# A graph attention layer with a mixer and a routed feed-forward block: the weighted sums over edges take pairs of neighbouring tiles, one accumulator, and one-hots that read their columns from PSUM

## The reference

```python
scores = einsum('ehd,ehd->eh', Q[dst], K[src] + 0.2 * rel[:, None, :]) / D ** 0.5
ex = exp(scores - segment_max(scores, dst)[dst])
denom = segment_sum(ex, dst)
agg = segment_sum(ex / denom[dst] * V[src], dst)      # 4 heads of 64
msgs = where(deg > 0, agg, V)
x = x + layernorm(msgs @ Wo + bo + xn) * gamma + beta + mixer(xn)
```

## Time and profile before

| | us |
|---|---|
| three runs: median | 2975.46 |
| lowest, highest | 2974.98, 2976.96 |
| the profiled execution: its time | 2994.86 |
| its span, first to last instruction | 2993.0 |
| first and last matmul of the weighted sums (start) | 1772.6, 2233.8 |
| mean granted TensorE clock, of full speed | 0.840 |

### The profile page before, as it was taken

How to read it: one execution, slowest core, us unless ns; L and a number is a source line. 1 busy time by engine, 2 the same in 40 slices (tenths; PEclk the granted TensorE clock), 3 DMA queues, 4 the chain that set the end, 5 groups by cost and what they waited for, 6 DMA issues and landing times. The chain is left out here.

```text
span 2993.0 us, 48887 instructions
## 1 busy us (share of the span) xinstructions
PE 2231.8 (75%) x11266; PEld 1389.1 (46%) x11267; DVE 1922.4 (64%) x3248; ACT 868.0 (29%) x2658; POOL 1478.5 (49%) x1460
## 2 busy tenths in 40 slices
PE   6863667666766766766676748999985999967997
PEld 3431333333333333333333436666654666546886
DVE  5653666666666666666666879999995666541111
ACT  2430011011101101100100177777761555531221
POOL 3555555555555555555555226666644434214442
PEclk9995777777777777777777779999997999978999
DMA  4545878787888788878778837777744444354541
GB/s 151 183 156 172 275 257 266 256 270 247 261 270 265 246 264 265 257 249 272 249 253 265 191 129 233 236 235 237 239 150 149 159 146 169 113 192 182 174 169 55
DMA packets 347414, 636.52 MB, mean 213 GB/s; under 512 B 36018, under 2 KB 224950, under 8 KB 347227
## 3 DMA queue, kind: packets, MB, share of 16 engines
q1 hardware_dynamic: 269259, 373.23, 37.9%
q0 software_dynamic: 77824, 262.55, 27.8%
q10 hardware_dynamic: 272, 0.00, 0.0%
HBM read 461.16 MB, written 175.42 MB: 213 GB/s over the span
## 5 line engine op out<-in xcount | busy, mean ns | idle before, releaser
L698 POOL DMA_INDIRECT s_kv<-kv_d,s_index x832 | 795.0, 956 | 657.6 <-issue 325.0
L829 PE MATMUL s_q_ps<-q,s_is_dst 128*128 x2496 | 511.7, 321 | 399.7 <-DVE s_key L752 272.5
L829 PEld LDWEIGHTS s_q_ps<-q,s_is_dst 128*128 128x128 bf16 x2496 | 210.6, 105 | 572.3 <-issue 506.5
L1190 PE MATMUL a_sum_ps<-a_w,a_is_dst 128*128 128x260 f32 x1664 | 421.8, 397 | 48.4 <-DVE odd_sums L1157 31.5
L748 DVE TENSOR_TENSOR s_key<-s_kv,s_rel_ps 128x1024 f32<-128x1024 f32 x208 | 252.4, 1214 | 230.1 <-remote 222.8
L1125 POOL TENSOR_TENSOR a_w<-a_v,a_w 128x512 f32<-128x512 f32 x208 | 284.7, 1369 | 225.2 <-ACT a_w L1095 173.0
L1190 PEld LDWEIGHTS a_sum_ps<-a_w,a_is_dst 128*128 128x128 f32 x1664 | 300.8, 190 | 169.3 <-DVE odd_sums L1157 123.2
L1103 ACT ACTIVATE a_w<-a_v,a_w 128x64 f32<-128x64 f32 x1248 | 319.9, 334 | 3.9 <-DMA a_v<-v_d 3.8
L834 PE MATMUL s_rel_ps<-rel,s_is_kind 64*128 64x64 bf16 x2496 | 244.7, 207 | 52.5 <-issue 51.9
L647 ACT COPY scores<-s_part 128x32 f32 (+1 forms) x104 | 22.6, 218 | 835.9 <-issue 708.6
L757 DVE TENSOR_REDUCE s_part<-s_key 128x16 f32<-128x1024 f32 x208 | 253.7, 1220 | 10.7
(11 more groups left out here) (295 smaller groups left out, 3030.4 us busy)
## 6 DMA issues: line engine op xcount, KB each, us to landing
v_d<-s_kv SPq DMA_DIRECT2D x208, 512.0 KB
a_v<-v_d SPq DMA_DIRECT2D x208, 512.0 KB, 5.3
s_local<-local_d SPq DMA_DIRECT2D x106, 256.0 KB
xh_d<-h_hid SPq DMA_DIRECT2D x24, 1024.0 KB, 6.9
s_kind<-type_d SPq DMA_DIRECT2D x212, 64.0 KB
s_kv<-kv_d,s_index POOLq DMA_INDIRECT x832
kv_d<-pkv SPq DMA_DIRECT2D x50, 256.0 KB, 2.0
wd<-in_L_ffn_Wd SPq DMA_DIRECT2D x8, 1024.0 KB, 12.2
```

The lines of the kernel that those rows point to most:

```text
L698: nc.gpsimd.indirect_dma_start(out=kv[:, g * GROUP + b, :], out_offset=None, in_=R["kv"], in_offset=bass.IndirectOffsetOnAxis(ap=index[:, ...
L829: nc.tensor.matmul(q_ps[b][:, u, :], is_dst[:, h, e], M["q3"][:, bass.ds(regs[g % GROUPS * GROUP + u], 1), j, :] .rearrange("p a c -> p (a ...
L1190: ins = nc.tensor.matmul(sum_ps[g % 2 * GROUP + u][:], is_dst[:, g % WRING, u, :], w[:, g % WRING, u, :], start=True, stop=True)
```

## The change

The unit of the weighted sums is now an *item*, two neighbouring tiles of one block; a block with an odd number of tiles gets an item whose second tile is the next block's. There is room for 440 items, so 220 groups of two items (880 tiles) where there were 208 of four tiles (832).

- Tile planning computes for each item its first tile and its block, by 15 small VectorE instructions that stand between the block table and the wait for the gathered edges, and stores both (`items`). TensorE turns the global node (`segment`) in place of `local`.
- `v_d` is laid out [partition, tile, 256] with room for 833 tiles, so that any two neighbouring tiles are 2 KB in a row of a partition. The scores stage writes the same 4 KB per partition and group, now 833 KB apart. The weighted sums load two tiles with each DMA, 256 KB, two DMAs per group, at an address from a register.
- The two matmuls of an item accumulate in one bank; there are four banks, and one add per item, always to `sums`. `odd`, its zeroing and the add at the end go.
- The one-hots are one instruction per tile, 128 x 128: column (from a copy in PSUM) minus global node, compared with minus the first node of the block. An edge of another block finds no column. Both scalars are addressed by registers.
- VectorE, ScalarE and SyncE load the item's tile numbers into registers in each group, two values at a time; VectorE has three such loads per group (blocks of group n, tiles and blocks of group n + 2), before it had one of four values.
- ScalarE multiplies two tiles in every fourth group and one in the others (before: in turn two and one), GpSimd the rest.
- The loops run over 27 times 8 groups, with 4 more behind.

```diff
--- before.py
+++ after.py
@@ -437,6 +451,9 @@
+            sp.wait_ge(S["items_set"], 2)
+            sp.dma_start(R["items"].rearrange("k (p c) -> p k c", p=IT_ROWS), item_i[:]).then_inc(S["table_in"], 16)
@@ -492,6 +511,26 @@
+            then(nc.vector.tensor_scalar(room_i[:], tiles[:], 1.0, None, ALU.add))
+            then(nc.vector.tensor_scalar(room_i[:], room_i[:], 1, None, ALU.arith_shift_right))
+            st.mark(nc.vector.memset(first_item[:, 0:1], 0.0))
+            then(nc.vector.tensor_copy(pairs[:], room_i[:]))
...
+            then(nc.vector.scalar_tensor_tensor(out=item_off[:], in0=first_item[:, 0:RBLK], scalar=-2.0,
...
+            then(nc.vector.scalar_tensor_tensor(out=item_tile[:], in0=item_no[:], scalar=2.0, in1=item_base[:],
+                                                op0=ALU.mult, op1=ALU.add))
+            nc.vector.tensor_scalar(item_i[:, 0, :], item_tile[:], float(T - 2), None, ALU.min).then_inc(S["items_set"], 1)
+            nc.vector.tensor_scalar(item_i[:, 1, :], item_blk[:], -1.0, None, ALU.add).then_inc(S["items_set"], 1)
@@ -525,7 +564,7 @@
-                x = src_f if b < 2 else local
+                x = src_f[:] if b < 2 else M["segment"][:].rearrange("p (t e) -> p t e", e=P)
@@ -610,8 +649,8 @@
-                        sp.dma_start(R["v"][bass.ds(i * (RING // 2) + h, 1)].rearrange("a p n -> (a p) n")
-                                     .rearrange("p (j c) -> p j c", c=C)[:, g % 2 * GROUP:(g % 2 + 1) * GROUP, :],
+                        sp.dma_start(R["v"][:, 0:T, :].rearrange("p (n u) c -> p n u c", u=GROUP)
+                                     [:, bass.ds(i * RING + g, 1)].rearrange("p a u c -> p (a u) c"),
@@ -948,14 +992,13 @@
-                zero(M["odd"], lo, hi)
+                zero(M["sums"], lo, hi)
...
-                zero(M["odd"], lo, hi)
-            zero(M["sums"], 0, RBLK)
+                zero(M["sums"], lo, hi)
@@ -1052,51 +1101,66 @@
...
-        TURNS = T // (VRING * GROUP)
+        PAIRS = GROUP // 2
+        BANKS = 4
+        NGROUP = ITEMS // PAIRS
+        TURNS, REST = NGROUP // VRING, NGROUP % VRING
...
-        sum_ps = [ctx.enter_context(nc.psum_tensor(f"a_sum_ps{b}", [P, AGG], F32)) for b in range(2 * GROUP)]
+        sum_ps = [ctx.enter_context(nc.psum_tensor(f"a_sum_ps{b}", [P, AGG], F32)) for b in range(BANKS)]
+        col_ps = ctx.enter_context(nc.psum_tensor("a_col_ps", [P, P], F32))
...
-        ACT_TILES = {g: range(0, 2 - g % 2) for g in range(VRING)}
-        POOL_TILES = {g: range(2 - g % 2, GROUP) for g in range(VRING)}
...
+        ACT_TILES = {g: range(0, 2 if g % 4 == 0 else 1) for g in range(VRING)}
+        POOL_TILES = {g: range(ACT_TILES[g].stop, GROUP) for g in range(VRING)}
...
+        tiles_of = lambda n: items[0:1, 0, bass.ds(n * PAIRS, PAIRS)]
+        blocks_of = lambda n: items[0:1, 1, bass.ds(n * PAIRS, PAIRS)]
...
+            at_tile = [sp.alloc_register(f"a_sp{k}") for k in range(PAIRS)]
+            def groups(i, count):
+                for g in range(count):
                     for name in ("pool_done", "act_done"):
                         sp.wait_ge(S[name], i * VRING + g + 1)
                     sp.nop(nofuse=True)
...
+                    regs = load_row(sp, at_tile, tiles_of(i * VRING + g), T - 2)
+                    for k in range(PAIRS):
+                        sp.dma_start(v[:, g, 2 * k:2 * k + 2, :], R["v"][:, bass.ds(regs[k], 2), :]).then_inc(v_in[g], 16)
...
+            def copy_scores(n, at):
+                regs = load_row(act, at_tile, tiles_of(n), T - 2)
+                for k in range(PAIRS):
+                    nc.scalar.copy(w[:, at, 2 * k:2 * k + 2, C:], scores[:, bass.ds(regs[k], 2), :]).then_inc(S["ex_ready"], 1)
...
+                        act.wait_ge(S["summed"], (n + 2) * PAIRS)
                         act.nop(nofuse=True)
...
+                        copy_scores(n + 1, (g + 1) % WRING)
+                    act.wait_ge(S["ex_ready"], (n + 1) * PAIRS)
+                    act.wait_ge(v_in[g], (i + 1) * (16 * PAIRS))
@@ -1105,100 +1169,104 @@
...
+            with pool.Fori(0, TURNS) as i:
+                groups(i, VRING)
+            groups(TURNS, REST)
...
+            nc.vector.tensor_copy(col_ps[:], M["col"][:]).then_inc(S["col_set"], 1)
...
-            dve.sem_inc(S["summed"], WRING)
...
+            dve.sem_inc(S["summed"], WRING * PAIRS)
...
-            def prepare(i, g):
...
-                dve.wait_ge(S["summed"], n + 1)
...
-                nc.vector.tensor_tensor(is_dst[:, g % WRING], M["col"][:, None, :].broadcast_to([P, GROUP, P]),
...
+            tile_at = [dve.alloc_register(f"a_tile{k}") for k in range(PAIRS)]
+            node_at = [dve.alloc_register(f"a_node{k}") for k in range(PAIRS)]
+            sums_at = [dve.alloc_register(f"a_sums{k}") for k in range(PAIRS)]
+            def ahead(n):
+                return (load_row(dve, tile_at, tiles_of(n), T - 2), load_row(dve, node_at, blocks_of(n), RBLK - 1))
+            def one_hot(at, k, tiles, blocks):
+                for u in range(2):
+                    ins = nc.vector.tensor_scalar(is_dst[:, at, 2 * k + u, :], col_ps[:],
+                                                  node_of[:, bass.ds(tiles[k] + u, 1)],
+                                                  M["first_node"][:, bass.ds(blocks[k], 1)], ALU.subtract, ALU.is_equal)
+                ins.then_inc(S["hot_done"], 1)
+            def groups(i, count, last):
+                for g in range(count):
                     n = i * VRING + g
-                    add(i, g, load_row(dve, at_block, M["blk"][0:1, bass.ds(n * GROUP, GROUP)], RBLK - 1))
+                    more = not (last and g + LEAD >= count)
+                    regs = load_row(dve, sums_at, blocks_of(n), RBLK - 1)
+                    if more:
+                        tiles, blocks = ahead(n + LEAD)
+                    for k in range(PAIRS):
+                        if more:
+                            dve.wait_ge(S["summed"], (n + LEAD + 1) * PAIRS)
+                            one_hot((g + LEAD) % WRING, k, tiles, blocks)
+                        j = n * PAIRS + k
+                        dve.wait_ge(S["summed"], j + 1 + WRING * PAIRS)
+                        dve.wait_ge(S["added"], j + BANKS)
+                        dve.nop(nofuse=True)
+                        at = sums[:, bass.ds(regs[k], 1), :].rearrange("p a c -> p (a c)")
+                        nc.vector.tensor_tensor(at, at, sum_ps[(g * PAIRS + k) % BANKS][:], ALU.add).then_inc(S["added"], 1)
...
-            dve.wait_ge(S["added"], T + 2 * GROUP)
-            nc.vector.tensor_tensor(sums[:], sums[:], odd[:], ALU.add).then_inc(S["whole"], 1)
...
+            with dve.Fori(0, TURNS) as i:
+                groups(i, VRING, False)
+            groups(TURNS, REST, True)
+            dve.wait_ge(S["added"], ITEMS + BANKS)
...
-                    pe.wait_ge(S["added"], n * GROUP + GROUP)
-                    for u in range(GROUP):
-                        ins = nc.tensor.matmul(sum_ps[g % 2 * GROUP + u][:], is_dst[:, g % WRING, u, :], w[:, g % WRING, u, :],
-                                               start=True, stop=True)
-                    ins.then_inc(S["summed"], 1)
+                    for k in range(PAIRS):
+                        pe.wait_ge(S["hot_done"], n * PAIRS + k + 1)
+                        pe.wait_ge(S["added"], n * PAIRS + k + 1)
+                        for u in range(2):
+                            ins = nc.tensor.matmul(sum_ps[(g * PAIRS + k) % BANKS][:], is_dst[:, g % WRING, 2 * k + u, :],
+                                                   w[:, g % WRING, 2 * k + u, :], start=(u == 0), stop=(u == 1))
+                        ins.then_inc(S["summed"], 1)
```

More of the change, by code:

```diff
@@ L37 @@
 T = TS_ROWS * TS_COLS
+ITEMS = 440
+IT_ROWS = 110
+IT_COLS = ITEMS // IT_ROWS
 EROWS, ECOLS = 125, 800
@@ L1040, in _, with load_row @@
             dve.wait_ge(S["back"], n_bank)
+def load_row(eng, regs, row, most):
+    eng.load(regs, row)
+    return [eng.snap(r, min_val=0, max_val=most) for r in regs]
 AGG = C + H
@@ L1116, in _, with groups @@
             pool.wait_ge(S["started"], 1)
-            with pool.Fori(0, TURNS) as i:
-                for g in range(VRING):
+            def groups(i, count):
+                for g in range(count):
                     n, tiles = i * VRING + g, POOL_TILES[g]
-                    pool.wait_ge(S["ex_ready"], n + 1)
-                    pool.wait_ge(v_in[g], (i + 1) * 16)
+                    pool.wait_ge(S["ex_ready"], (n + 1) * PAIRS)
+                    pool.wait_ge(v_in[g], (i + 1) * (16 * PAIRS))
                     pool.nop(nofuse=True)
@@ L1159, in _ @@
-            at_block = [dve.alloc_register(f"a_at{u}") for u in range(GROUP)]
-            LEAD = 2
-            def groups(i, last):
-                for g in range(VRING):
-                    if not (last and g + LEAD >= VRING):
-                        prepare(i, g + LEAD)
-                    n = i * VRING + g
```

(13 more changed lines are left out.)

121 lines of the change are left out of this document (61 added, 60 removed).

## The result

The kernel after takes 3279.1 us (median of 4 runs, 3275.6 to 3282.7), the kernel before 2976.2 beside it: ratio 1.102, 95% interval 1.100 to 1.103, **+303 us**. The forecast was 3149 (3040 to 3260): the right side and the right engine, but 130 us short and out of the range.

A forecast was written before the change was run, and what follows sets the result against it. VectorE's queue was taken to bound the weighted sums, at 2.94 us a group: +186 for the stage, -13.4 for the last add, +0.8 for the later start, +173 us in all, from 2975.5 to 3149 us (3040 to 3260).

The forecast's parts named there:

- VectorE's queue bounds, in both kernels: Weighted sums: VectorE's instruction queue sets the pace, 2.94 us a group after the change, +186 us; chance 0.70.
- Issue: Sign for the forecast: "issue", VectorE's own queue, stands ahead of its instructions over a large part of the sums.
- VectorE waiting for PE: Sign against the forecast, in the sums: VectorE waiting for PE (TensorE), ACT or DMA.
- Three loads, 1.45 us: VectorE's queue, per group: three loads of two values at 0.48 us each, 1.45 in all, bounds 1.05 and 1.95.
- 0.60 + 0.71 + 0.18 = 1.49: VectorE's queue, us per group: four one-hots 0.60, two adds and thresholds 0.71, loop's end and stalls 0.18.
- The last add -13.4: End of the sums: the final add, beside which nothing runs, goes and saves 13.4 us.
- tile planning 0: Fifteen small VectorE instructions, some 4 us, are hidden in the 12.8 us wait for the gathered edges: no cost.
- zeroing 0: ScalarE loses 10.8 us of zeroing that ended just as its first exponential was called for: 0 gained.
- scores stage 0: Scores stage writes the same rows at another pitch: 0 taken, between 10 us gained and 33 us lost.
- B, TensorE bounds: Sums: VectorE's queue is short or runs ahead, TensorE bounds at 1.90 us a group, 2920 us; chance 0.12.
- C, ScalarE bounds: Sums: VectorE's queue comes out at its low end, ScalarE's 2.26 us a group bounds, 2999 us; chance 0.08.
- D, the clock: Sums: TensorE, working 64%, falls to 1.2 GHz half of the time, +62 us, 3211 us; chance 0.10.

The follow-up runs named there:

- e5: Kernel after, with VectorE making one aligned load of four values per group and keeping the blocks in registers until their adds: 3002.2 us, ratio 1.003 to kernel before.
- e6: Kernel before, with VectorE's one load of four block numbers per group split into two loads of two, all used: 3162.5 us, ratio 1.057.
- e1: Kernel after, with two more unused loads per group on SyncE; these were missing from the program that ran, so it is the kernel after on another chip: 2908.2 us.
- e2: Kernel before, with two more unused loads per group on VectorE; these were missing from the program that ran, so it is the kernel before: 2605.0 us, ratio 1.000.
- e10: Kernel after with one aligned load of four, kept blocks, and one-hots comparing columns in SBUF instead of PSUM: 2732.5 us, ratio 1.050 to kernel before.
- e11: Kernel after with one aligned load of four, kept blocks, and VectorE's loop unrolled to 16 groups: 2683.6 us, ratio 1.032 to kernel before.

## Why the prediction was right and wrong

*VectorE's queue bounds, in both kernels: right.* Shown by e5 and e6 from both sides: loads added to the old kernel cost it what their rows say, and loads taken from the new one give it back. One sign did not come, though. "Issue" was to stand ahead of VectorE's instructions, and VectorE waiting for PE was to speak against the forecast; the profile has 323 us of idle time ahead of the one-hots put down to PE and 12 to "issue". By that sign alone the theory would have been dropped, and it was the sign that was wrong.

*Three loads, 1.45 us: this step failed.* It took a load of two for 0.21 us, on a line of 64 ns per value through TensorE's 4 and 16 values. Both of those are aligned fours, one step and four; they say 0.26 us per step and nothing of a load that is none. Measured: 0.53, so 3 x (0.53 - 0.34) more than even a load of four, and 2.05 us for the phase, past the upper end of 1.95. The loads alone are 3 x (0.53 - 0.21) = 0.96 us longer than forecast; 0.36 of that came back, since no address is computed for each load (27 in the whole stage), and unpackings and gaps are shorter than taken. What is left is 0.60 us more than the 1.45, 132 us over 220 groups: the whole of the 130 that were missing. The upper bound, "0.65 (as now)", took a load of four as the most that a load of two can cost, and had no row for that.

The Trainium skill, "Runtime: NRT & Kernel Launch", section "Instruction fetch mechanics", has a figure: about 200 ns per register. By it two values take 0.4 us as an estimate and the forecast 3149 + 220 x 3 x 0.19 = 3274. The runs agree for SyncE's loads that are no aligned fours, 0.20 us per value beside a fixed 0.07; VectorE's load of two takes more, 0.53, and an aligned four takes far less, 0.32.

*The rest of the group, 0.60 + 0.71 + 0.18 = 1.49: right in the sum*, measured 1.49, and with some luck: one-hots and adds take 3.46 - 2.05 = 1.41 us inside a turn and not 1.31, and the turn's end some 0.08 a group and not 0.18. The one-hots from PSUM took 0.40 and not 0.20 each, but start 0.32 apart and lie beside the queue, so it cost nothing. The 0.26 us that the prediction has for one, an estimate from a table of the Trainium skill, "VectorE: DVE Perf Modes", section "The TRN2 errata — SBUF-src ops pay a fixed extra latency per instruction", is below the measured value too.

*The last add -13.4, tile planning 0, zeroing 0, scores stage 0: right in the sum.* The stage's +303.2 against +302.9 in the medians leaves nothing for them together; tile planning and zeroing were not tried singly. The row pitch showed no cost: from the first to the last write of values are 1441.6 us before and 1429.6 after, and on the chip of e1 and e2 1063.8 and 1060.9.

*B, TensorE bounds:* fell. TensorE was busy 61% and waited. Register work does not hide here, whatever the queue holds: VectorE's engine stands idle for 1.43 us in the three loads. With the loads gone e5 runs at 2.21 us a group, still over B's 1.90.

*C, ScalarE bounds:* fell; its load, too, is 0.49, and it still waits 317 of 550 us. *D, the clock:* fell; with TensorE busy 61% the granted clock of the sums was 0.97, nearly all at its 2.4 GHz level, and the 0.75 of the scores stage did not come.

## What to carry to other kernels

Count the instructions of an engine's queue like those of its engine, register loads first, and measure the very size and alignment that the change will use: pack what a group needs into one aligned row of 16 bytes, and keep it in registers rather than load it again. A ring of waits in which every engine waits for the next names no culprit, and the profile may put a full queue down to another engine; look for the hole in one engine's timeline, and then at its queue's rows. When an added cost shows no effect, look in the trace whether the added instructions are there at all. When a reverse test gives the number that was expected, look at what else moved in it.

## What the runs showed of the hardware, unexpected

- A register load costs 0.07 us + 0.20 us per value, or 0.10 + 0.22 per aligned 16 bytes (SyncE). Two values cost more than four: 0.47 against 0.32, on VectorE 0.53 against 0.34.
- A one-hot of 128 columns with all operands in SBUF (0.34 us) waits for GpSimd's running multiply and so takes up to 1.65 us (e10); from PSUM it takes 0.40 and never waited in 880 (e5). The one-hot of 128 x 512 from SBUF waits likewise, 1.400 us on the mean in place of 0.695 (e6).
- A loop of 340 instructions on VectorE's queue stands still for 6.1 to 7.9 us between two turns and fetches code (e11); loops of 171 to 198 don't.
- The kernel before runs its sums in the same 461.2 and 461.4 us in two profiles (before and e2), and differs by 380 us in the scores stage, where the stretch from 400 to 1300 us moved 260 GB/s in the one and 349 in the other. By that they ran on unlike chips; what makes these differ was not tried.
